# A graph layer's second hidden state turned by transposing DMA instead of TensorE, on one Trainium2 core

## The reference

```python
edge_index = jnp.stack([src, dst])
h = jnp.maximum(_layernorm(x), 0.0)
x = x + _L0_gnn_ref(h, edge_index, Wq, bq, Wk, bk, Wv, bv)   # masked attention
h = jnp.maximum(_layernorm(x), 0.0)
x = x + _L1_gnn_ref(h, W1, b1, gamma, beta, W2, b2, edge_index)

def _L0_gnn_ref(...):            # q = x @ Wq + bq, k and v alike
    adj = zeros((N, N)).at[src, dst].set(1.0)
    a = q @ k.T / sqrt(512)
    a = a * adj + (1.0 - adj) * -1e6
    return softmax(a) @ v

def _L1_gnn_ref(...):            # agg: weighted sum over edges and self loops
    h = agg(x @ W1 + b1)
    h = relu(gamma * (h - mu) * rsqrt(var + 1e-5) + beta)    # over the nodes
    return agg(h @ W2 + b2)
```

## Time and profile before

| | |
|---|---|
| median of 3 runs (lowest to highest) | 326.31 us (326.1 to 327.01) |
| the profiled execution's own time | 325.77 us |
| its span, first to last instruction | 323.9 us |
| mean granted TensorE clock | 0.999 of full speed |
| PE busy | 309.1 us, 95% of the span, 1402 matmuls |
| PEld, DVE, ACT, POOL busy | 238.5, 209.7, 120.5, 57.7 us |
| DMA moved | 19.04 MB, 23.0% of 16 engines' span on the hardware queue |

### The profile page before, as it was taken

How to read it: one execution, slowest core, us unless ns; L and a number is a source line. 1 busy time by engine, 2 the same in 40 slices (tenths; PEclk the granted TensorE clock), 3 DMA queues, 4 the chain that set the end, 5 groups by cost and what they waited for, 6 DMA issues and landing times.

```text
span 323.9 us, 4758 instructions
## 1 busy us (share of the span) xinstructions
PE 309.1 (95%) x1402; PEld 238.5 (74%) x1402; DVE 209.7 (65%) x464; ACT 120.5 (37%) x191; POOL 57.7 (18%) x96
## 2 busy tenths in 40 slices
PE   1899889999999999999999999999999999999995
PEld 0677456577666678888888888888888888888884
DVE  6899999996849725655667765566731178458311
ACT  1917223434473433515243445326503023524000
POOL 5103000000000054612225343020210015200000
PEclk9999999999999999999999999999999999999999
DMA  7911200000321030392715143131400000000131
GB/s 221 314 66 58 74 0 1 1 2 0 132 85 46 2 65 0 66 233 61 114 40 108 32 99 70 27 66 24 75 0 2 0 1 2 0 0 2 61 136 67
DMA packets 34374, 19.04 MB, mean 59 GB/s; under 512 B 28080, under 2 KB 28336, under 8 KB 34352
## 3 DMA queue, kind: packets, MB, share of 16 engines
q1 hardware_dynamic: 34352, 18.76, 23.0%
HBM read 10.36 MB, written 2.10 MB: 38 GB/s over the span
## 4 chain that ended last, share of the span: by engine, by line
PE 83%; DVE 8%; issue 3%; DVEq 3%; ACT 1%; DMA 1%; POOL 0%; SPq 0%; POOLq 0%
PE ps L842 19%; PE ps L844 18%; PE ps L843 18%; PE ps L1107 9%; PE ps L1029 9%; PE ps L904 7%; DVE src_oh L634 3%; DVEq L634 1%; DVE dst_oh L636 1%; PE ps L990 1%; DVE wA L594 1%; DMA xt<-x_in 1%; DVE bnst L553 1%; PE ps L870 1%; DVEq L623 1%
## 5 line engine op out<-in xcount | busy, mean ns | idle before, releaser
L634 DVE TENSOR_SCALAR src_oh<-iota,ecol 128x512 f16 x172 | 48.9, 349 | 0.7 <-PE ps L904 0.6
L904 PE MATMUL ps<-src_oh,dst_oh 128*128 x172 | 41.7, 381 | 2.8 <-DVE dst_oh L636 2.8
L405 ACT ACTIVATE cnt<-ps 64x512 int16<-64x512 f32 x32 | 18.9, 591 | 36.1 <-PE ps L909 35.7
L904 PEld LDWEIGHTS ps<-src_oh,dst_oh 128*128 x172 | 18.3, 114 | 19.0 <-issue 7.4
L1029 PE MATMUL ps<-cnt,qh 128*128 128x512 f32 x128 | 29.9, 390 | 0.0
L1107 PE MATMUL ps<-qh,cnt 128*128 128x512 f32 x128 | 29.3, 390 | 0.0
L1107 PEld LDWEIGHTS ps<-qh,cnt 128*128 128x128 f32 x128 | 24.0, 188 | 5.2 <-DVE vb L823 0.3
L1029 PEld LDWEIGHTS ps<-cnt,qh 128*128 128x128 f32 x128 | 23.9, 188 | 5.1 <-issue 0.2
L842 PE MATMUL ps<-kT,qh 128*128 128x512 f32 x64 | 25.4, 397 | 0.0
L842 PE MATMUL ps<-v,pT 128*128 128x512 f32 x64 | 25.2, 393 | 0.0
L844 PE MATMUL ps<-v,pT 128*128 128x512 f32 x64 | 25.0, 391 | 0.0
(11 more groups left out here) (150 smaller groups left out, 608.8 us busy)
## 6 DMA issues: line engine op xcount, KB each, us to landing
xt<-x_in SPq DMA_DIRECT2D x16, 256.0 KB, 3.2
out<-xt SPq DMA_DIRECT2D x8, 256.0 KB, 3.0
wA_raw<-L_gnn_Wk_in SPq DMA_DIRECT2D x2, 512.0 KB, 6.6
wB_raw<-L_gnn_Wv_in SPq DMA_DIRECT2D x2, 512.0 KB, 8.1
wA_raw<-L_gnn_Wq_in SPq DMA_DIRECT2D x2, 512.0 KB, 3.7
wB_raw<-L_gnn_W_in SPq DMA_DIRECT2D x2, 512.0 KB, 3.8
w_raw<-L_gnn_W_in SPq DMA_DIRECT2D x2, 512.0 KB, 4.9
bias_row<-L_gnn_b_in SPq DMA_DIRECT2D x2, 256.0 KB, 4.4
```

The source lines that it names most:

```text
L405: act.activation(cnt16[rows, a * KC:(a + 1) * KC, w // 2, :], ps[a * WIN:(a + 1) * WIN, i % 2, :].rearrange("p (s n) -> p s n", n=P), ACT. ...
L634: dve.tensor_scalar(src_oh[:, bass.ds(slot, 1), j, :].rearrange("p a n -> p (a n)"), iota[:, :], ecol[:, bass.ds(c + j, 1)], None, ALU.is_ ...
L904: m = pe.matmul(ps[:, i % 2, :], dst_oh[:, bass.ds(slot, 1), :, j].rearrange("p a n -> p (a n)"), src_oh[:, bass.ds(slot, 1), j, :].rearra ...
```

## The change

TensorE no longer turns `ht`. ACT writes `h16[:, 0]` = fp16(2048 ht) (`h16_hi`), DVE writes `h16[:, 1]` = fp16(2048 ht - high) (`h16_lo`), SP turns each plane (128x512, half the size of a plane of probabilities) by a transposing DMA into `h16T` (`turn_h2`), and `h2T_hi` (ACT) and `h2T_lo` (DVE) widen them from SBUF. Bank 6 and the fp32 transposes (8 times 4) go. To make room, `pT` becomes single buffered, so `p_hi(t)` and `p_lo(t)` wait for `weighted_v(t-1)`. On ACT `p_hi` moves ahead of `h2_relu`, and in steps 3 to 7 `h1_hi` moves behind the exponential; on DVE `h1_tmp` and `h1_lo` move behind the mask. W2's split leaves POOL and steps 3 and 4: ACT makes both high halves in step 8, DVE both low halves in step 9.

```diff
-    hT, pT, w2, _, w2_raw, g32 = shared(
+    hT, pT, h16, h16T, _, w2, _, w2_raw, g32 = shared(
         [("hT", [P, 2, KC, N], F32R)],
-        [("pT", [P, 2, 2, NT, P], F32R), ("w2", [P, 2, KC, D], F32R)],
+        [("pT", [P, 2, NT, P], F32R), ("h16", [P, 2, D], F16), ("h16T", [P, 2, KC, P], F16), ("unused", [P, 2 * D], F32),
+         ("w2", [P, 2, KC, D], F32R)],
         [("pT_place", [P, 2, 2, NT, P], F32R), ("w2_raw", [P, 2, KC, D], F32)],
...
+        def turn_h2(t, part, split, done, landed):
+            sp.wait_ge(S[split], t + 1)
+            if t >= 1:
+                sp.wait_ge(S[done], t)
+            sp.dma_start_transpose(h16T[:, part, :, :], h16[:, part, :]).then_inc(S[landed], 16)
         for t in range(ADJ):
             turn_counts(t)
-        for t in range(NT):
-            turn_p(t, 0, "p16_hi", "p_hi", "p16_hi_in")
-            turn_p(t, 1, "p16_lo", "p_lo", "p16_lo_in")
+        for t in range(NT + 1):
+            if t < NT:
+                turn_p(t, 0, "p16_hi", "p_hi", "p16_hi_in")
+                turn_p(t, 1, "p16_lo", "p_lo", "p16_lo_in")
             if t == 0:
...
                 turn_counts(t + ADJ)
+            if t >= 1:
+                turn_h2(t - 1, 0, "h16_hi", "h2T_hi", "h16_hi_in")
+                turn_h2(t - 1, 1, "h16_lo", "h2T_lo", "h16_lo_in")
         sp.wait_ge(S["xb_ready"], NT)
...
                 add_bv(t + XT)
-            if 0 <= t - 1 < LOADS:
-                split_w(4, (t - 1,))
...
             act.wait_ge(S["p16_hi_in"], 16 * (t + 1))
-            if t >= 2:
-                act.wait_ge(S["pv_ps"], t - 1)
-            act.activation(pT[:, t % 2, 0, :, :], p16T[:, 0, :, :], ACT.Copy, scale=1.0 / P_UNIT).then_inc(S["p_hi"], 1)
+            if t >= 1:
+                act.wait_ge(S["pv_ps"], t)
+            act.activation(pT[:, 0, :, :], p16T[:, 0, :, :], ACT.Copy, scale=1.0 / P_UNIT).then_inc(S["p_hi"], 1)
...
             if t >= 1:
-                act.wait_ge(S["h2T_ps"], t)
+                act.wait_ge(S["h16_lo"], t)
             act.activation(ht[:, :], x1[:, t, :], ACT.Relu, bias=lnb[:, 2, t:t + 1],
...
         def h2T_hi(t):
-            act.wait_ge(S["h2T_ps"], t + 1)
+            act.wait_ge(S["h16_hi_in"], 16 * (t + 1))
             if t >= 1:
                 act.wait_ge(S["w1_ps"], t)
-            act.activation(hnT[:, 0, :], bank(6), ACT.Copy).then_inc(S["h2T_hi"], 1)
+            act.activation(hnT[:, 0, :], h16T[:, 0, :, :].rearrange("p k n -> p (k n)"), ACT.Copy,
+                           scale=1.0 / H_UNIT).then_inc(S["h2T_hi"], 1)
+        def h16_hi(t):
+            act.wait_ge(S["h2_ready"], t + 1)
+            if t >= 1:
+                act.wait_ge(S["h16_hi_in"], 16 * t)
+            act.activation(h16[:, 0, :], ht[:, :], ACT.Copy, scale=H_UNIT).then_inc(S["h16_hi"], 1)
...
         for i in range(NT + 3):
-            if i >= 3:
+            if i >= NT:
                 h1_hi(i - 3)
                 count_parts(ACT_COUNTS[3:])
+            if 2 <= i <= NT:
+                p_hi(i - 1)
             if 2 <= i <= NT + 1:
                 h2_relu(i - 2)
-            if 2 <= i <= NT:
-                p_hi(i - 1)
+                h16_hi(i - 2)
             if 2 <= i <= NT + 1:
...
                 p_hi(0)
+            if 3 <= i < NT:
+                h1_hi(i - 3)
             if i < NT:
...
                                ACT.Copy).then_inc(S["bc_ready"], 1)
-            if 0 <= i - 3 < LOADS:
-                split_w(4, (i - 3,))
+            if i == NT:
+                split_w(4)
             if i == NT - 1:
...
             dve.wait_ge(S["p16_lo_in"], 16 * (t + 1))
-            if t >= 2:
-                dve.wait_ge(S["pv_ps"], t - 1)
-            dve.tensor_scalar(pT[:, t % 2, 1, :, :], p16T[:, 1, :, :], 1.0 / P_UNIT, None, ALU.mult).then_inc(S["p_lo"], 1)
+            if t >= 1:
+                dve.wait_ge(S["pv_ps"], t)
+            dve.tensor_scalar(pT[:, 1, :, :], p16T[:, 1, :, :], 1.0 / P_UNIT, None, ALU.mult).then_inc(S["p_lo"], 1)
...
         def h2T_lo(t):
-            dve.wait_ge(S["h2T_hi"], t + 1)
-            dve.tensor_tensor(hnT[:, 1, :], bank(6), hnT[:, 0, :].bitcast(F32), ALU.subtract).then_inc(S["h2T_lo"], 1)
+            dve.wait_ge(S["h16_lo_in"], 16 * (t + 1))
+            if t >= 1:
+                dve.wait_ge(S["w1_ps"], t)
+            dve.tensor_scalar(hnT[:, 1, :], h16T[:, 1, :, :].rearrange("p k n -> p (k n)"), 1.0 / H_UNIT, None,
+                              ALU.mult).then_inc(S["h2T_lo"], 1)
+        def h16_lo(t):
+            dve.wait_ge(S["h16_hi"], t + 1)
+            if t >= 1:
+                dve.wait_ge(S["h16_lo_in"], 16 * t)
+            dve.scalar_tensor_tensor(out=h16[:, 1, :], in0=ht[:, :], scalar=H_UNIT, in1=h16[:, 0, :], op0=ALU.mult,
+                                     op1=ALU.subtract).then_inc(S["h16_lo"], 1)
...
         for i in range(NT + 3):
-            if i >= 3:
+            if i >= NT:
                 h1_tmp(i - 3)
...
                 p_lo(i - 1)
+            if 2 <= i <= NT + 1:
+                h16_lo(i - 2)
             if i == NT:
...
                 add_loops(i)
+            if 3 <= i < NT:
+                h1_tmp(i - 3)
             if 2 <= i <= NT + 1:
                 h2T_lo(i - 2)
+            if i == NT + 1:
+                split_w(4, 0)
+                split_w(4, 1)
+            if 3 <= i < NT:
+                h1_lo(i - 3)
             if i == 0:
...
                 for k in range(KC):
-                    if (n, k) == (1, KC - 1) and t >= 2:
-                        h2_turn(t - 2)
                     m = three(bank(2 * (t % 2) + n), lambda a: qh[:, t, a, k * P:(k + 1) * P],
...
             for k in range(NT):
-                m = three(bank(4), lambda a: pT[:, t % 2, a, k, :], lambda a: v[:, k, a, :], k == 0, k == NT - 1)
+                m = three(bank(4), lambda a: pT[:, a, k, :], lambda a: v[:, k, a, :], k == 0, k == NT - 1)
             m.then_inc(S["pv_ps"], 1)
-        def h2_turn(t):
-            pe.wait_ge(S["h2_ready"], t + 1)
-            if t == 0:
-                pe.wait_ge(S["item_lo"], nth(("q", 1, 2)))
-            if t >= 1:
-                pe.wait_ge(S["h2T_lo"], t)
-            for k in range(KC):
-                m = pe.transpose(bank(6)[:, k * P:(k + 1) * P], ht[:, k * P:(k + 1) * P], ident[:, :])
-            m.then_inc(S["h2T_ps"], 1)
         def times_w1(t):
+            pe.wait_ge(S["h2T_hi"], t + 1)
             pe.wait_ge(S["h2T_lo"], t + 1)
...
             agg1((0, 1), (d,))
-        h2_turn(NT - 2)
         weighted_v(NT - 1)
...
         agg1((2, 3), early)
-        h2_turn(NT - 1)
+        pe.wait_ge(S["x1_ready"], NT)
         pe.wait_ge(S["dinv_ready"], 1)
...
-        pe.wait_ge(S["wp_lo"], 2 * LOADS)
+        pe.wait_ge(S["w_lo"], 4 * LOADS)
         for k in range(2):
```

More of the change, by code:

```diff
@@ L35 @@
 P_UNIT = 32768.0
+H_UNIT = 2048.0
 EXACT = 4096.0
@@ L152, in gnn_kernel @@
     s_ps mask_set masked top_ready exp_done rinv_ready p16_hi p16_lo p16_hi_in p16_lo_in p_hi p_lo pv_ps xb_ready x1_ready
-    bn_ready ln2_coef h2_ready h2T_ps h2T_hi h2T_lo w1_ps h1_tmp h1_hi h1_lo
+    bn_ready ln2_coef h2_ready h16_hi h16_lo h16_hi_in h16_lo_in h2T_hi h2T_lo w1_ps h1_tmp h1_hi h1_lo
     cnt_act cnt_dve bc_ps bc_ready agg1_ps g_ready g_stats z_coef z_ready z_hi z_lo
```

## The result

The changed kernel takes 323.1 us as the median of 5 runs (322.56 to 324.58) against 326.84 (326.1 to 327.06) for the kernel before beside it. The ratio is 0.9909, with a 95% interval of 0.9893 to 0.9926: 2.4 to 3.5 us less, 3.0 in the middle. (The quotient of the two medians alone would be 3.7 us; I go by the ratio and its interval.) The profiled execution took 322.66 us with a span of 320.8.

A forecast was written before the change was run, and what follows sets the result against it. TensorE, busy 309.1 of 323.9 us and never waiting in the loop, was taken as the bound. Gain 3.52 less a 0.5 wait gave 3.0 us, so 322.8 profiled and 323.3 as median; range 322.4 to 325.2.

The forecast's parts named there:

- The gain, 8 x 0.44: TensorE, attention loop and behind it: eight turns of `ht` leave its queue, 0.44 us each, 3.52 us in all.
- The wait at block 3, 0.5: Way out of the loop: TensorE's early aggregation waits about 0.5 us for ACT's late cast of count block 3.
- the 0.2 of spare: Early aggregation before the change: TensorE reached count block 3 with 0.2 us to spare after ACT's cast.
- The sum, 3.0: Whole kernel: 3.52 gained less 0.5 of wait gives 3.0 us less.
- The forecast of 322.8 for the profiled execution: Whole kernel: the profiled execution, 325.77 us before, would take 322.8.
- The loop hides the new work: Attention loop: the new ACT, DVE and DMA work costs zero, with about 1 us of cover at three places.
- The landing of a half plane, 3.3 with its hand-over: Transposing DMAs of the `h16` planes in the loop: each assumed to take 3.3 us, bounds nothing and 5.8.
- the turn of block 6: Behind the loop: `h2T_lo(6)` done by 238.8, `times_w1(6)` starting at 239.0; zero cost, upper bound 2.4 us.
- W2's split moved: no gain, since `p_lo` was in time even so: Loop steps with POOL's split: `p16_lo` stretched from 1.23 to 2.45 us, `p_lo` still in time; moving it gains nothing.
- The slower rival: DVE in the loop: late low plane delays `weighted_v` from a 5.0 us landing on; 328.1 us at 5.8; 12%.
- The price by the Trainium skill: TensorE's removed transposes: about 275 ns each, 32 x 0.275 = 8.8 us in all.
- the rival of 318.0: TensorE: turns cost the skill's price because the chain hides fill time in the matmuls around them; 318.0 us; 2%.

The follow-up runs named there:

- cast_first: Changed kernel with ACT's cast of count block 3 put ahead of `h1_hi(5)`: 322.42 us, 0.9894 of the kernel before.
- turn_twice: Kernel before with each of TensorE's eight turns of `ht` done twice in place, same result: 329.32 us, 1.0094 of the kernel before.
- h1_first: Changed kernel with `h1_tmp`, `h1_hi` and `h1_lo` back at the start of each step: 322.48 us, 0.9895 of the kernel before.
- no_turn: Changed kernel without the sixteen DMA turns of `h16`, the unturned planes being widened: 322.52 us, 0.9881 of the kernel before.
- lo_late_3: Changed kernel with three idle transposing DMAs between the high and low plane's turns, low plane 3.7 us later: 331.32 us, 1.0148 of the kernel before.

## Why the prediction was right, and where its steps were not

- **The gain, 8 x 0.44**: right in mechanism, a little small. cast_first, which has no wait, ends 3.9 us earlier than the kernel before by the ruler (183.1 against 187.0), which is 0.49 for each turn. The period shrinks by 0.47 or 0.48, and turn_twice adds 0.45 for each set. The few hundredths for each turn beyond the transposes' 0.44 are not explained by any run.
- **The wait at block 3, 0.5**: right in place, releaser and cause, and 0.54 by size. h1_first shows the cause and cast_first that nothing takes its place. That the size came out so well is in part luck. Against TensorE's first early matmul the residual starts 0.52 later than before the change and ACT's cast 0.51, where the prediction had 0.7; of the 0.2 of spare that it took off, 0.14 go into the hand-over from the cast's end (228.76 in the chain) to the matmul; and 0.09 more are lost behind the restart.
- **The sum, 3.0**: 3.9 - 0.5 = 3.3 by the ruler, and 3.0 by the ratio, with an interval of 2.4 to 3.5 that holds both. The forecast of 322.8 for the profiled execution met 322.66.
- **The loop hides the new work**: right. `p_lo` has 202.89 - 201.87 = 1.0 to spare, as worked out; the high plane's widening ends at 204.2 and the exponential comes at 206.0. In no_turn's trace the DMAs are free.
- **The landing of a half plane, 3.3 with its hand-over**: too long. It is 2.5, with the hand-over: ACT's `h16_hi` of block 6 is over at 231.1 and `h2T_hi` starts at 233.59. This is why the turn of block 6, which I had just in time, has room: `h2T_lo(6)` ends at 235.3, `times_w1(6)` starts at 236.25. Block 7 has 0.9 as well.
- **W2's split moved: no gain, since `p_lo` was in time even so**: wrong. That was true of the old period and the old place of ACT's cast. I read the cover (0.4 us, 176.30 against 176.72) in the trace of before and did not carry it into the changed kernel, where the period is 0.46 shorter and the cast 0.5 later. Left in place the split costs 1.4 us, and still 0.8 when the cast is where it was. The sum did not suffer, because the change moved it.
- **The slower rival**: its form was right, a late low plane turns the gain into a loss, and so was its limit: it had a landing of 5.0 us, and 2.5 of landing with about 2.5 of delay is 5.0. The place was not. I had DVE's ring (its round of instructions in a step) and `weighted_v` as the first to suffer; it is `times_w1`. Beyond it, 1.3 us of delay made the periods 14.8 to 15.2 instead of 13.7, about one for one in each step. The first block, which costs 4.4 of lo_late_3's 9.2, is not in the prediction.
- **The price by the Trainium skill** (TensorE: Matmul & The Clock Gate, Part 4: PE-mode transpose), 0.275 for each bf16 transpose of 128x128: the runs show 0.09 to 0.11 for one of fp32 in a row of four, so the rival of 318.0 falls.

## What to carry to other kernels

When TensorE never waits, count what leaves its queue by the distance between starts, and then follow every other engine's program through one shortened period: each cover in the old trace shrinks by what the period loses and by what is put ahead of it, and a collision that was free before can be the next bound. Look hardest at the ends of the loop, where moved instructions no longer overlap with a full step. When changes are bundled, take them apart: here the turn carried the gain, the new places of h1 cost 0.5 to 0.7 us by the traces, and the move of W2 avoided a collision that cost 0.8 already and that they had made dearer, 1.4.

## What the runs showed of the hardware that I had not expected

In lo_late_3 the first wait was 2.55 us long by its row (2.7 by the distance between starts), and it cost more than its length. The profile's windows show the granted TensorE clock (the PEclk column, behind the busy times of the engines), and the timeline of PE the same matmuls:

```profile
154.00:156.60 2.60, 0.06 (x1) 0.02 (x1) 0.52 (x2) 0.33 (x1) 0.00 (x0) 1.00 0.49 99
156.60:158.00 1.40, 1.39 (x6) 1.12 (x7) 1.33 (x3) 0.01 (x1) 0.00 (x0) 0.90 0.63 117
158.00:159.00 1.00, 1.00 (x4) 0.81 (x3) 0.96 (x2) 1.00 (x1) 0.80 (x1) 0.50 0.00 0
159.00:160.00 1.00, 1.00 (x3) 0.79 (x3) 0.45 (x2) 0.05 (x1) 0.92 (x2) 0.50 0.00 0
...
161.00:164.00 3.00, 3.00 (x14) 2.48 (x13) 1.30 (x2) 0.93 (x2) 0.33 (x1) 0.98 1.07 226
...
157.38 0.39 PE L895 MATMUL ps<-wB,hnT 128*128 128x512 f32 x1
...
158.36 0.63 PE L895 MATMUL ps<-wB,hnT 128*128 128x512 f32 x1
158.79 0.63 PE L896 MATMUL ps<-wB,hnT 128*128 128x512 f32 x1
```

TensorE idled from 154.1 to 156.6 at full grant, started again at full speed, and fell to half (1.2 GHz) about 1 us later, for some 3 us: the distance between matmuls went from 0.23 to 0.43. `times_w1` took 4.3 us instead of 2.8. The later waits of 1.1 to 1.4 us left the clock at 2.4 GHz. The idle stretch of 2.5 us was thus followed by another 1.5 us of loss in `times_w1`; the wait and what followed it are most of the first block's 4.4. It was seen in one profile.

DVE's instruction with two SBUF inputs and POOL's subtraction did not share: in three kernels, twice in each, `p16_lo` ended 1.1 us after POOL did, whatever the overlap (2.44 to 2.93 long).
